# Node degrees summed in four column groups of the array, and a guarded block of 120 products parted into six

## The reference

```python
# layer 0
msg = xn[edge_index[0]]
agg = jax.ops.segment_sum(msg, edge_index[1], num_segments=N)
deg = jax.ops.segment_sum(jnp.ones((E,), x.dtype), edge_index[1], num_segments=N)
agg = agg / jnp.maximum(deg, 1.0)[:, None]
conv_out = jax.nn.relu(agg @ W_conv + b_conv)
# ... attention over all 1250 nodes' first 256 rows, and a batch norm over nodes
# layer 1
agg = jax.ops.segment_sum(x[src], dst, num_segments=N)
h = (1.0 + eps) * x + agg
h = jax.nn.relu(batch_norm(h @ W1 + b1, g1, be1))
h = h @ W2 + b2
h = jax.nn.relu(batch_norm(h, g2, be2))
return x + h
```

## Time and profile before

| | |
|---|---|
| median of 3 runs | 365.75 us (365.27 to 365.75) |
| the profiled execution's own time | 365.71 us |
| its span | 363.9 us |
| TensorE busy | 349.3 us, 96% of the span |
| granted TensorE clock, mean | 0.997 of full |

### The profile page before, as it was taken

The page is one execution under the profiler, slowest core; times in us unless marked ns, Lnnn a source line. Parts: engine busy times, 40 slices in busy tenths (PEclk is TensorE's granted clock), DMA queues, the critical chain, the costliest instruction groups (busy, mean ns, idle before and its releaser), DMA issues.

```text
span 363.9 us, 6197 instructions
## 1 busy us (share of the span) xinstructions
PE 349.3 (96%) x2072; PEld 224.6 (62%) x2072; DVE 245.2 (67%) x666; ACT 181.7 (50%) x303; POOL 94.1 (26%) x163
## 2 busy tenths in 40 slices
PE   8999899989999999999998999999999999999994
PEld 4678655757777666767565675455555555565562
DVE  5889999998998995867996886522464453422325
ACT  0548538768477167454437766411533644233132
POOL 8132020000000000100042778722277465101100
PEclk9999999999999999999999999999999999999998
DMA  6990303300000000034900000000000000010223
GB/s 179 283 304 19 119 1 119 118 3 1 3 3 4 3 3 3 3 103 145 263 7 3 0 2 3 2 2 1 2 0 0 2 0 2 0 51 21 70 58 85
DMA packets 13539, 18.05 MB, mean 50 GB/s; under 512 B 1839, under 2 KB 6895, under 8 KB 13491
## 3 DMA queue, kind: packets, MB, share of 16 engines
q1 hardware_dynamic: 12538, 17.21, 16.3%
q10 hardware_dynamic: 953, 0.23, 0.3%
HBM read 14.88 MB, written 2.56 MB: 48 GB/s over the span
## 4 chain that ended last, share of the span: by engine, by line
PE 82%; DVE 6%; ACT 5%; issue 3%; POOL 2%; DMA 1%; DVEq 0%; SPq 0%; ACTq 0%; POOLq 0%
PE bank L1436 78%; PE bank L1466 2%; PE bank L1834 1%; POOL ln_s L491 1%; ACT hn L688 1%; PE bank L1793 1%; DVE st_row L1324 1%; ACT hh L832 1%; ACT sqr L694 1%; DMA edge<-src 1%; DVE x L1387 0%; PE bank L1647 0%; ACT hring L602 0%; DVE aggf L1344 0%; DVE hl L1305 0%
## 5 line engine op out<-in xcount | busy, mean ns | idle before, releaser
L1436 PE MATMUL bank<-AT,hh 125*128 125x400 f16 (+3 forms) x250 | 81.1, 332 | 1.0 <-DVE hl L1305 0.5
L1436 PE MATMUL bank<-AT,hl 125*128 125x400 f16 (+3 forms) x250 | 80.8, 331 | 0.0
L994 DVE TENSOR_SCALAR ring<-iota_code,code 125x250 f16<-125x250 f16 x200 | 46.1, 306 | 1.4 <-issue 1.4
L1436 PEld LDWEIGHTS bank<-AT,hh 125*128 125x128 f16 x250 | 24.1, 97 | 19.2 <-issue 1.1
L1436 PEld LDWEIGHTS bank<-AT,hl 125*128 125x128 f16 x250 | 24.2, 97 | 17.7 <-issue 0.2
L1436 PE MATMUL bank<-ring,S 125*128 125x250 f16 x200 | 33.5, 310 | 0.0
L1436 PE MATMUL bank<-a_hi,w_hi 128*128 128x400 f16 (+1 forms) x96 | 32.6, 339 | 0.0
L1436 PE MATMUL bank<-agg_hi,w_hi 128*128 128x400 f16 (+1 forms) x96 | 32.6, 339 | 0.0
L1436 PE MATMUL bank<-agg_hi,w_lo 128*128 128x400 f16 (+1 forms) x96 | 32.5, 338 | 0.0
L1436 PE MATMUL bank<-a_hi,w_lo 128*128 128x400 f16 (+1 forms) x96 | 32.5, 338 | 0.0
L1436 PE MATMUL bank<-agg_lo,w_hi 128*128 128x400 f16 (+1 forms) x96 | 32.5, 338 | 0.0
(11 more groups left out here) (236 smaller groups left out, 704.2 us busy)
## 6 DMA issues: line engine op xcount, KB each, us to landing
w_s<-w SPq DMA_DIRECT2D x4, 1024.0 KB, 5.0
x_in<-x SPq DMA_DIRECT2D x5, 448.0 KB
x<-x SPq DMA_DIRECT2D x2, 1120.0 KB
out<-x SPq DMA_DIRECT2D x6, 224.0 KB
wB<-wk SPq DMA_DIRECT2D x1, 1024.0 KB, 9.3
wA<-wq SPq DMA_DIRECT2D x1, 1024.0 KB, 14.3
wC<-w_conv SPq DMA_DIRECT2D x1, 1024.0 KB, 16.0
wB<-wv SPq DMA_DIRECT2D x1, 1024.0 KB, 6.0
```

Source lines behind the costliest of these rows:

```text
L994: return dve.tensor_scalar(ring[:, slot, j, a:b], iota_code[0:CH, a:b], code[:, bass.ds(c + j, 1)], float(-CODES * t), ALU.subtract, ALU.i ...
L1436: return pe.matmul(o, l, r, start=start, stop=stop, skip_group_check=True)
```

## The change

The degree sums get a stationary operand of 32 columns instead of 128. The columns of a block are cut into four quarters (`quarters`: 113 of 450, or 100 of 400), and the quarter g is summed into output partitions 32g to 32g+31 of the bank, so there are 40 products of 113 or 100 columns for the ten of 450 or 400. The order is four quarters for tile 0, the branch (with 40 guarded products for ten), and then 36. VectorE makes the reciprocals of the quarters in a small tile `rdq` (128 by 113). A new piece `E<c>` then spreads them: four float32 products, whose stationary operand is column 32g of the identity repeated 128 times, write quarter g into all 128 partitions of a bank, and ScalarE copies that to `rdb`. TensorE waits for the reciprocals before `E` (`s_rdq`); VectorE waits for the copy before the first `A` that uses it (`s_rdb`).

`D0` moves one slot up, `D1` too, `D2` to the head of `LAST`; `E0` and `E1` stand two places later, `E2` behind `A02`. The banks of `LAST` are dealt anew. `agg1_extra` goes, and its 120 products become six branches of 20, each ahead of the last two products of its sum in `agg1_rows`.

```diff
-    "MX2 G8", "QT2 G9", "KV2 UK3 D0", "O2 UQ3 A00", "A10", "MX3 A20", "QT3 A30 F1", "KV3 D1 A01",
+    "MX2 G8", "QT2 G9 D0", "KV2 UK3 E0", "O2 UQ3 A00", "A10", "MX3 A20", "QT3 A30 F1 D1", "KV3 A01 E1",
...
+def quarters(c):
+    c0, w = COLS[c]
+    q = -(-w // 4)
+    return [min(g * q, w - q) for g in range(4)], q
...
-LAST = "A31 F2 D2 A02 A12 A22 A32 A33".split()
+LAST = "D2 A31 F2 A02 E2 A12 A22 A32 A33".split()
...
-LAST_BANKS = (6, 4, 0, 1, 2, 3, 7, 5)
+LAST_BANKS = (0, 6, 4, 1, 5, 2, 3, 7, 0)
...
-                if name[0] == "D":
-                    free_group(copy(rdb[:, c0:c0 + w], ps[:, 0:w]), name)
+                if name[0] == "E":
+                    act.activation(rdb[:, c0:c0 + w], ps[:, 0:w], ACT.Copy).then_inc(sem("s_rdb"), 1)
+                    act.wait_ge(sem("s_rdb"), c + 1)
+                    act.sem_inc(free[PLACE[name][0]], 1)
...
             weight_mean(1)
+            counts_out("E2")
...
+                    ps = read_group(dve, name)[:, 0:quarters(c)[1]]
+                    if c:
+                        dve.wait_ge(full[PLACE[f"E{c - 1}"][0]], PLACE[f"E{c - 1}"][1] + 1)
                     own.step(dve.tensor_scalar(d, ps, 1.0, wscale[:, 0:1], ALU.max, ALU.mult))
-                    n_deg[0] = own.mark(dve.reciprocal(d, d))
+                    dve.reciprocal(d, d).then_inc(sem("s_rdq"), 1)
...
-                    ins = accumulate([(ps[:, 0:w], [(ones16[0:L, :], AT[:, k, c0:c0 + w]) for k in range(T)],
-                                       [(ones16[0:L, :], ATlo[:, k, c0:c0 + w]) for k in range(T)])])[0]
+                    starts, w = quarters(int(name[1]))
+                    places = [ps[g * 32:(g + 1) * 32, 0:w] for g in range(4)]
+                    blocks = [slice(c0 + s, c0 + s + w) for s in starts]
+                    ins = sum_up([[(o, ones16[0:L, 0:32], AT[:, k, b]) for o, b in zip(places, blocks)] for k in range(T)],
+                                 [(o, ones16[0:L, 0:32], ATlo[:, k, b]) for k in range(T) for o, b in zip(places, blocks)])
+                elif name[0] == "E":
+                    c = int(name[1])
+                    starts, w = quarters(c)
+                    pe.wait_ge(sem("s_rdq"), c + 1)
+                    ps = open_group(pe, name)
+                    for g, s in enumerate(starts):
+                        ins = mm(ps[:, s:s + w], ident[:, 32 * g:32 * g + 1].broadcast_to([P, P]), rdq[:, 0:w], True, True)
...
+                    if k == T - 1:
+                        with pe.If_lt(big_r, most_r):
+                            for j in range(T):
+                                for h in (hh, hl):
+                                    mm(ps[:, 0:w], h[:, j, fs], ATlo[:, j, c0:c0 + w], False, False)
+                        pe.end_ifs()
```

More of the change, by code:

```diff
@@ L322, in gnn_kernel @@
         rdb = place("rdb", [P, N], F32, 146)
+        rdq = place("rdq", [P, -(-COLS[0][1] // 4)], F32, 152)
         x1 = place("x1", [L, T, D], F32, 154)
@@ L765, in _ @@
                         conv_high(int(name[1]))
-                    elif name[0] in "AD":
+                    elif name[0] in "AE":
                         counts_out(name)
+                    elif name[0] == "D":
+                        pass
                     else:
@@ L1039, in attention @@
                 elif name[0] == "D":
-                    c0, w = COLS[int(name[1])]
+                    c = int(name[1])
+                    d = rdq[:, 0:quarters(c)[1]]
                     dve.wait_ge(sem("s_bn1"), 1)
[L1042 to L1047, removed]
+                    ps = read_group(dve, name)[:, 0:quarters(c)[1]]
+                    if c:
+                        dve.wait_ge(full[PLACE[f"E{c - 1}"][0]], PLACE[f"E{c - 1}"][1] + 1)
                     own.step(dve.tensor_scalar(d, ps, 1.0, wscale[:, 0:1], ALU.max, ALU.mult))
-                    n_deg[0] = own.mark(dve.reciprocal(d, d))
-                    if name in LAST:
-                        dve.sem_inc(free[PLACE[name][0]], 1)
+                    dve.reciprocal(d, d).then_inc(sem("s_rdq"), 1)
+                    dve.sem_inc(free[PLACE[name][0]], 1)
+                elif name[0] == "E":
+                    pass
                 elif name[:2] == "WO":
@@ L1062, in attention @@
                     dve.sem_inc(free[PLACE[name][0]], 1)
-            n_deg = [0]
             def weight_low(layer, half):
@@ L1189, in mean_rows @@
                 units[0] += 1
-                own.after(n_deg[0])
+                dve.wait_ge(sem("s_rdb"), ci + 1 if ci < NC else NC)
                 if name in RAW:
@@ L1694, in accumulate, with sum_up @@
                 return last
+            def sum_up(steps, extra):
+                for o, l, r in steps[0]:
+                    mm(o, l, r, True, False)
+                with pe.If_lt(big_r, most_r):
+                    for o, l, r in extra:
+                        mm(o, l, r, False, False)
+                pe.end_ifs()
+                for n, step in enumerate(steps[1:]):
+                    for o, l, r in step:
+                        ins = mm(o, l, r, False, n == len(steps) - 2)
+                return ins
             seen = pe.alloc_register("seen")
@@ L1759, in agg1_rows @@
                         close_group(ins, name)
[L1761 to L1771, removed]
             def y_done(i, f):
@@ L1804, in _ @@
                 turn_rows(i, hring1, 3, "s_hb", f"g{i}")
-                if i == T - 1:
-                    agg1_extra()
                 agg1_rows(i)
```

## The result

The kernel before takes 365.7 us (median of 13 runs, 365.27 to 365.85), the changed one 366.27 us (13 runs, 365.8 to 367.22). The ratio is 1.0024, with a 95% interval of 1.0017 to 1.0032: slower by a quarter of a per cent (the two medians alone are 0.57 us apart, or 1.0016). I had added up 0.37 us less and called it no change that can be measured. The span of the profiled execution went from 363.9 to 364.9 us; its own time is 366.77 us, half a microsecond above the median of its kernel, and the spans of the 13 executions go from 364.0 to 365.4.

What follows compares the result with a forecast made beforehand. TensorE was taken to bound the degree-sum stretch; removing 5.31 us of sums and adding 2.24 for narrow sums and 2.70 for spreading gave −0.37 us, so 365.3 us, range 364.4 to 367.0.

Steps and rivals of the forecast that it cites:

- E0: Spreading of the first degree sum's reciprocals: 0.90 us, turn at 118.33 us, reciprocals ready 0.7 us early, no wait.
- E1: Spreading of the second degree sum's reciprocals: 0.90 us, twenty wide products more in between than the first, no wait.
- E2: Spreading of the third degree sum's reciprocals: 0.90 us, turn at 178.44 us, reciprocals ready half a microsecond early, no wait.
- The branches: Second layer's last tile: six branches for one gain 0 and lose 0, bounds −0.3 and +0.5 us.
- the twelve are all started by 228.6: Last tile: TensorE's twelve products all start by 228.6 us, 0.6 us ahead of its next group at 229.22.
- My own sign of being wrong: Wrong if a degree sum takes over 1.1 us, or if the stretch behind 190 us changes its length.
- Rival D: Last tile: the branches are on the path after all, −0.3 us on top, 365.0 us; chance 0.07.
- B: Degree sums: the four short blocks do not overlap, +3.1 us, 368.8 us (half lost: 367.2); chance 0.15.
- C: At the first or third spreading TensorE waits for VectorE's quarters, 0.5 to 1.2 us, 365.8 to 366.5 us; chance 0.10.
- The sums: Three degree sums in narrow form: four blocks overlap, 0.78 us for the first, 0.73 each for the others, 2.24 in all.
- The spreading: Spreading after each degree sum: eight float32 passes each, 0.90 us apiece, 2.70 us for all three.
- The sum: Whole kernel: −5.31 + 2.24 + 2.70 = −0.37 us, 365.3 us, no change that can be measured; chance 0.45.

Runs made afterwards that it cites:

- the branches alone: The kernel before with its one branch over 120 products parted into six, nothing else: 365.43 us, ratio 0.9999.
- 64 products: The changed kernel with 64 unexecuted products of zeros (128 instructions) in the third degree sum's always-skipped block: 365.61 us, ratio 1.0000.
- the order of `undo_w`: `undo_w` ahead of the last tile's low half on VectorE: 365.38 us on the kernel before; 365.13 us on the changed kernel with 64 unexecuted products.
- the kernel before moved: The kernel before with 76 unexecuted products of zeros (152 instructions) in the third degree sum's always-skipped block: 370.13 us, ratio 1.0119.
- the degrees alone: The changed kernel with the old single branch over 120 products put back: 368.86 us, ratio 1.0070.

## Why the prediction was wrong, point by point

- **The branches: wrong, and this decides.** I priced the six branches between −0.3 and +0.5 us and took 0. They are worth 0 in themselves (the branches alone: 0.9999). What I left out, and so put at nothing without a reason, is that a branch also moves TensorE on in its instruction stream, and that code added elsewhere shifts that stream against its blocks. The change adds instructions to TensorE ahead of the second layer. The last tile, where 240 instructions are skipped within 2 us, then lay so that TensorE stood still for 1.57 us: +1.03 us in the profiled execution, 0.57 us by the medians. Moving the code by 16, 32 or 128 instructions takes the pause away in the profiled execution, by 256 it returns, and moving the kernel before brings it there. That the place of the code decides is shown by these runs; that TensorE waits for a block of instructions rests on the period, the packet counts and the packet 2.2 to 2.4 us ahead of each restart. The words "the twelve are all started by 228.6" are the step that failed; two of them started at 229.90 and 230.08. My own sign of being wrong came true with it: the stretch behind 190 us changed its length. And TensorE did not start within 0.2 us of `hl`, but 0.42 us behind its end, as in the kernel before; the shorter first skip gave 0.12 us only in kernels without the pause.
- **Rival D and the others.** None holds this. B (no overlap), which carried most of my chance of slower, is refuted by the forty products in 0.56 to 0.79 us; C (a new wait at E) by E0 and E2 without any idle time; D by the wait for `aggf` in the branches alone and with 64 products.
- **The sums: the mechanism right, the size short.** The forecast was 0.78 + 0.73 + 0.73 = 2.24 us. D0 costs 114.38 − 113.50 = 0.88 (G9's last product starts at 113.28 and takes 0.22). The long row at 160.47 for 160.43 gives D0 and D1 together 3.61 + 0.04 − 1.85 = 1.80 us (3.61 removed, 1.85 for E0 and E1), so D1 is 0.92 (read directly it is 0.85: the window behind it starts at 144.78 for 143.93, so these subtractions hold to 0.07). From there to A32's multiply the change gains 0.16, so D2 is 1.70 − 0.16 − 0.87 = 0.67. Together 2.47, which is 0.23 more. The chain has a piece of it: 0.10 and 0.15 us of "issue" between D0 or D1 and the window behind it, which D2 does not have. So D2 came out 0.06 under my 0.73, and the two that stand ahead of a window 0.10 and 0.19 over; I had given all three the same 0.13 us for entering and leaving the narrow form. Why it costs more there, no run shows.
- **The spreading: right.** 2.72 us (0.98 and twice 0.87) for 2.70.
- **The cover of E: right, though thinner at E2** (0.3 us for 0.5).
- **VectorE's 6 us: right.** Its busy time falls from 245.2 to 239.1 us, and the time does not.
- **The sum** without the pause would have been −0.12 us, and the kernel with 64 products says that much: span 363.8 for 363.9, ratio 1.0000. "No change that can be measured" was thus the right answer for the work that is executed; where the code that is not executed lies, the whole argument did not ask.

## What to carry to other kernels

Where an engine's code holds many skipped instructions close together, any edit to that engine's code, even far ahead of it, can make or remove a pause of one to two microseconds; if a change gains or loses for no reason in its own stretch, compare the "issue" pieces of the chain, and shift the code by a few unexecuted instructions before judging the edit. A gain that ends in another engine's wait is only worth having together with the edit that removes that wait: here the order of `undo_w`. And when a sum moves to another bank or place, ask what the pieces it leaps over had been covering.

## What the runs showed of the hardware

- The pause of TensorE at the last tile lasts 1.1 to 2.0 us and appears as "issue" in the chain of waits. With six branches one of them is far longer than its fellows (2232 ns for 217); with one branch its own duration tells nothing (325 ns with and without the pause). The Trainium skill (Runtime: NRT & Kernel Launch, Instruction fetch mechanics) says that instructions come in blocks of 256, fetched in order, and that a taken branch to a block that is not loaded must wait for a fetch. The period of 256 agrees, and so do the packets of 16 KB. The Trainium skill (the same section) also says that the fetch is hidden by the pace of issue; here it was not where 240 instructions were skipped within 2 us.
- A pause can cost more than itself. After 2.02 us (four of the twelve products done) TensorE was granted 0.68 and 0.63 in the next stretches, and after 1.66 us (six done, the kernel before moved) 0.50 for 3 us; after 1.57 and 1.11 us (ten done), and after the 1.45 us at 179.69, it was 1.00. Where the clock fell, the last tile cost 3.2 us (the degrees alone) and 2.8 us (the kernel before moved); the changed kernel and the one with 256 instructions lost 0.6 and 1.0 us. Whether the length decides or what TensorE did just before, no run separates.
- Four float16 products of 32 output columns each, on the same rows of the array, run beside each other: 40 of 100 columns in 0.56 us from their first start to the next product's (0.67 us with what the entry costs, by the subtraction above), against 1.70 us for ten of 400 columns.
